# Second layer's query product: two 64-row tiles per head pair instead of one 128-row tile with a block-diagonal matrix

## The reference, cut to what matters

```python
xn = _ln(x, ln_w, ln_b)
q = softmax((xn @ Wq + bq).reshape(b, t, h, dh), axis=-1)
k = softmax((xn @ Wk + bk + (1.0 - src_mask) * -1e6).reshape(b, t, h, dh), axis=1)
v = ((xn @ Wv + bv) * src_mask).reshape(b, t, h, dh)
att = jnp.einsum('bnhd,bnhl->bhdl', k, v)          # 64 x 64 per head
y = jnp.einsum('bnhd,bhdl->bnhl', q, att).reshape(b, t, d)
scale, shift = jnp.split((silu(emb) @ W_emb + b_emb)[:, None, :], 2, axis=2)
hh = _ln(y, ln2_w, ln2_b) * (1.0 + scale) + shift
return x + silu(hh) @ W_out + b_out
```

## Time and profile before

| | us |
|---|---|
| median of 3 runs | 2306.27 |
| lowest, highest of the 3 | 2303.68, 2310.38 |
| the profiled execution, its own time | 2308.4 |
| its span, first to last instruction | 2306.6 |
| granted clock of PE over the span, share of full | 0.959 |

### The profile page before, as it was taken

The page is one execution under the profiler, slowest core; times in us unless marked ns, Lnnn a source line. Parts: engine busy times, 40 slices in busy tenths (PEclk is TensorE's granted clock), DMA queues, the critical chain, the costliest instruction groups (busy, mean ns, idle before and its releaser), DMA issues. The chain is left out here.

```text
span 2306.6 us, 30566 instructions
## 1 busy us (share of the span) xinstructions
PE 2144.4 (93%) x10240; PEld 1401.8 (61%) x10240; DVE 2044.7 (89%) x2254; ACT 1606.9 (70%) x3119; POOL 1776.2 (77%) x1046
## 2 busy tenths in 40 slices
PE   9889989988998899899979998998977899999999
PEld 3345555555555555555545555555545588888878
DVE  4899999999999999999999999999999666666666
ACT  3677787887777778777777787777656355566655
POOL 0587899999999999999999999999999522233325
PEclk9889999999999999999999999998978999999999
DMA  6611231141114111521331141114001201121113
GB/s 217 256 40 53 84 141 46 51 173 57 44 53 170 51 51 46 174 92 55 99 122 46 56 157 63 42 51 175 33 28 53 94 27 35 33 63 60 40 55 129
DMA packets 86139, 191.20 MB, mean 83 GB/s; under 512 B 8350, under 2 KB 11678, under 8 KB 85983
## 3 DMA queue, kind: packets, MB, share of 16 engines
q1 hardware_dynamic: 85982, 189.25, 24.7%
HBM read 171.91 MB, written 17.30 MB: 82 GB/s over the span
## 5 line engine op out<-in xcount | busy, mean ns | idle before, releaser
L1464 POOL TENSOR_TENSOR arena<-arena 128x1024 f32<-128x1024 f32 x512 | 1201.1, 2365 | 118.1 <-ACT arena L624 116.0
L1059 DVE TENSOR_TENSOR_SCAN arena<-ps,arena 128x512 f32<-128x512 f32 x1024 | 1235.1, 1246 | 16.4 <-ACT ps L624 13.5
L624 ACT ACTIVATE ps<-arena 128x512 f32<-128x512 f32 x1087 | 717.0, 676 | 270.9 <-DVE arena L1059 184.7
L339 PEld LDWEIGHTS ps<-keep,arena 128*128 128x128 f32 x4096 | 493.7, 147 | 262.1 <-issue 133.7
L339 PE MATMUL ps<-keep,arena 128*128 128x128 f32 x4096 | 550.3, 285 | 94.1 <-POOL arena L1464 88.4
L1044 DVE TENSOR_TENSOR arena<-ps,arena 128x1024 f32<-128x1024 f32 x407 | 487.0, 1197 | 25.3 <-PE ps L339 23.2
L278 PE MATMUL ps<-arena 128*128 128x512 f32 x1024 | 470.8, 605 | 17.8 <-issue 17.1
L278 PEld LDWEIGHTS ps<-arena 128*128 128x128 f32 x1024 | 190.3, 195 | 220.2 <-issue 219.7
L624 ACT ACTIVATE arena<-ps 128x512 f32<-128x512 f32 (+2 forms) x393 | 198.5, 538 | 135.3 <-PE ps L278 65.9
L1431 POOL TENSOR_TENSOR arena<-arena 128x1024 f32<-128x1024 f32 x105 | 248.2, 2364 | 15.1 <-PE ps L339 15.0
L624 ACT ACTIVATE arena<-arena 128x2 f32<-128x2 f32 (+4 forms) x662 | 238.3, 365 | 25.7 <-POOL arena L1408 7.5
(11 more groups left out here) (147 smaller groups left out, 2707.6 us busy)
## 6 DMA issues: line engine op xcount, KB each, us to landing
arena<-scr_bc SPq DMA_DIRECT2D x128, 512.0 KB, 7.2
arena<-in_inT SPq DMA_DIRECT2D x184, 256.0 KB, 2.7
arena<-in_x SPq DMA_DIRECT2D x17, 512.0 KB, 3.7
scr_x<-arena SPq DMA_DIRECT2D x32, 256.0 KB, 2.0
arena_b<-scr_x SPq DMA_DIRECT2D x16, 512.0 KB, 3.7
arena_c<-scr_x SPq DMA_DIRECT2D x32, 256.0 KB, 2.9
out<-arena_c SPq DMA_DIRECT2D x32, 256.0 KB, 2.1
arena<-in_x SPq DMA_DIRECT2D x30, 256.0 KB, 3.3
```

The source lines that it names most:

```text
L339: last = e.matmul(YP[:, 128 * q:128 * q + 128], hb[G % R][:, i, 128 * q:128 * q + 128], ident, start=(g == 0 and i == 0 and q == 0), stop= ...
L624: return e.activation(o_, i_, f, **kw)
L1059: e.tensor_tensor_scan(H, DA[s % 4], H, h0, MUL, ADD).then_inc(v_sc)
L1464: e.tensor_tensor(H, H, Ct[:, GN * g:GN * g + GN, :], MUL).then_inc(g_w)
```

## The change

`att` keeps only the two heads' matrices, 64 columns wide: rows 0 to 63 are the even head, rows 64 to 127 the odd head. The zeroing on POOL and its semaphore go. `attention` writes `att` in one instruction of 128 partitions where there were two of 64. `y_mm` issues two products for each `f` of a tile, one per head: 64 partitions of `qT` by 128 tokens as the stationary operand, 64 by 64 of `att` as the moving one. The heads of a pair go to different banks: one bank holds the even heads of both tiles, the other the odd heads. `y_block` scales one bank (both tiles, one parity of heads) per instruction, and waits first for both tiles' products.

```diff
-        qT, acc, att, kb = sb(4, 18 * 128), sb(4, 64), sb(4, 128), [sb(4, TB) for _ in range(2)]
+        qT, acc, att, kb = sb(4, 18 * 128), sb(4, 64), sb(4, 64), [sb(4, TB) for _ in range(2)]
             def y_mm(K):
-                e.wait_ge(v_att, 2 * (K // 8 + 1))
+                e.wait_ge(v_att, K // 8 + 1)
                 e.wait_ge(a_qT, 2 * K + 2)
+                P = [bank8(("y", K, h), (v_y, 2 * K + h + 1)) for h in range(2)]
                 for t in (2 * K, 2 * K + 1):
-                    P, at_ = bank8(("y", t), (v_y, t + 1)), 128 * (t % 18)
+                    at_, to = 128 * (t % 18), 256 * (t % 2)
                     for f in range(4):
-                        last = e.matmul(P[:, 128 * f:128 * f + 128], qT[:, f, at_:at_ + 128], att[:, f, :], start=True, stop=True)
+                        for h in range(2):
+                            head = slice(64 * h, 64 * h + 64)
+                            last = e.matmul(P[h][:, to + 64 * f:to + 64 * f + 64], qT[head, f, at_:at_ + 128], att[head, f, :],
+                                            start=True, stop=True)
                     last.then_inc(p_ya)
             def attention(b):
-                e.wait_ge(g_att, 1)
                 if b:
                     e.wait_ge(p_ya, 16)
-                for lo in (0, 64):
-                    rows_ = slice(lo, lo + 64)
-                    e.tensor_tensor(att[rows_, :, rows_], acc[rows_, :, :], ks[rows_, :].unsqueeze(2).broadcast_to([64, 4, 64]),
-                                    MUL).then_inc(v_att)
+                e.tensor_tensor(att, acc, ks.unsqueeze(2).broadcast_to([128, 4, 64]), MUL).then_inc(v_att)
             def y_block(K):
-                for n in range(2):
-                    t = 2 * K + n
-                    e.wait_ge(p_ya, t + 1)
-                    e.tensor_tensor(yt[:, n, :].rearrange("p (a b) -> p a b", a=8),
-                                    PS[bank_of["y", t]].rearrange("p (a b) -> p a b", a=8),
-                                    rq[:, t, :].unsqueeze(2).broadcast_to([128, 8, 64]), MUL).then_inc(v_y)
+                e.wait_ge(p_ya, 2 * K + 2)
+                for h in range(2):
+                    e.tensor_tensor(yt.rearrange("p n (a h b) -> p n a h b", a=4, h=2)[:, :, :, h, :],
+                                    PS[bank_of["y", K, h]].rearrange("p (n a b) -> p n a b", n=2, a=4),
+                                    rq[:, 2 * K:2 * K + 2, :].rearrange("p n (a h) -> p n a h", h=2)[:, :, :, h].unsqueeze(3)
+                                    .broadcast_to([128, 2, 4, 64]), MUL).then_inc(v_y)
-                if n == 2:
-
-                    e.wait_ge(p_op, 256)
-                    e.memset(flat(att), 0.0).then_inc(g_att)
```

More of the change, by code:

```diff
@@ L149, in program @@
         g_c, g_r1, g_r2, g_r3, g_rs, g_nm, g_dt, g_du, g_gw, g_w = (sem("g_" + n) for n in ("c", "r1", "r2", "r3", "rs", "nm", "dt", "du", "gw", "w"))
-        g_att, g_m1, g_mask, g_l1, g_l2, g_lrs, g_q, g_xo = (sem("g_" + n) for n in ("att", "m1", "mask", "l1", "l2", "lrs", "q", "xo"))
+        g_m1, g_mask, g_l1, g_l2, g_lrs, g_q, g_xo = (sem("g_" + n) for n in ("m1", "mask", "l1", "l2", "lrs", "q", "xo"))
         after = lambda k, n: ((16 * k[0] + k[1] + n) // 16, (k[1] + n) % 16)
```

## The result

| | us |
|---|---|
| changed kernel, median of 9 runs | 2312.68 (2310.79 to 2316.67) |
| before, median of 9 runs | 2306.27 (2302.68 to 2310.38) |
| ratio, 95% interval | 1.0026 (1.0017 to 1.0036) |
| span of the profiled execution, after and before | 2310.9 and 2306.6 |

The changed kernel is slower by 6.4 us by the medians (by the interval, 3.9 to 8.3 us). The forecast was 2310.4: 4.1 us slower.

A forecast was written before the change was run, and what follows sets the result against it. PE was taken as the bound in the stretch with nearly all changed calls; 12 y_mm calls on the chain at +0.29 us plus 0.6 in the last pass gave +4.1, so 2310.4 us, range 2299 to 2323.

The forecast's parts named there:

- The stream of records: y_mm on PE: 32 half-row records, pairs side by side at 0.112 us, 1.79 us in all, as today.
- B: Rival in y_mm: one load at a time, a call 3.80 us, +2.02; 2336 us in all; chance 0.14.
- D: Rival in y_mm: a load waits for the product in its own rows, a call +1.11 us; 2322 us; chance 0.08.
- C: Rival in y_mm: half the rows halve the load, a call -0.60 us; 2300 us; chance 0.09.
- The change of division: PE around each y_mm: emptying the array, going in and out, an exposed load; 0.28 us, making a call +0.29.
- The four calls in the gaps: y_mm(7) to y_mm(10), where PE sits idle for something else: the dearer calls add nothing to the end.
- The last pass: At h_tr(15), after the later y_block: PE waits about 0.6 us for ACT's normalisation, once.
- The cover in the other passes: Running passes: the later y_block is covered, as DVE sits idle 1.18 to 3.79 us for L553 before it.
- Edits that cost nothing: attention in one instruction, the dropped zeroing (0.53 us on POOL) and bank8's wait for both banks: no effect on the time.
- The sum: Whole kernel: 12 x 0.29 + 0.6 = +4.1 us, laid on the median of 2306.27: 2310.4 us.

The follow-up runs named there:

- the quarters: Changed kernel with each y_mm product cut again by tokens, loading 64 rows by 64 columns: 2300.04 us against 2307.41 for the kernel before, ratio 0.9967.
- the two filled kernels: Kernel before and changed kernel, each with three fp32 products of 512 columns added where PE waits ahead of o_mm(8): 2305.41 and 2310.45 us.

## Why the prediction was right

**The stream of records.** The forecast was 0.056 us from record to record, with both row halves side by side and nothing gained. It is 0.056, so B (0.11), D (0.08) and C (0.03) are out. This decides more than the time does: the stated range, 2299 to 2323, held C and D as well. The reason holds as well: with half the moving columns a record still costs 0.108 us, and the load binds. L256, with 2 rows and 2 moving columns, had been the row that said so the earlier trace rows, and the overlap of row halves could be taken over from the column halves of `kv_mm`.

**What the argument left out.** I wrote that the moving side had been hidden behind the weights. It is not hidden but nearly equal: with 64-column loads and 128 moving columns a pair costs 0.109 us, with 128-column loads and 64 moving columns a record 0.108. The change halved one of two equal limits. Halving both is what pays, and the quarters do that with one more cut.

**The change of division.** Forecast was a call dearer by 0.29 us. It is 0.34 in the blocks up to `y_mm(6)`, 0.33 in the passes, and 0.31 where the change of division was bought alone. Taken 12 times, this term was too small by 0.6 us of 4.1, within its bounds of 0.23 to 0.5. The four calls in the gaps added nothing, as forecast (0.92 us late at `o_mm(8)` against 0.91 before them).

**The last pass.** Forecast 0.6 us of waiting at `h_tr(15)`, measured 0.55; in the kernel that has the later start alone it is 0.72, and the stretch is longer by 0.69. The cover in the other passes held.

**Edits that cost nothing.** `attention(1)` takes 0.93 us in one instruction against 2.39 in two, and the first low part of block 7 then waits 0.87 us for ACT, so nothing was passed on. Behind 2000 us PE shows waits for DVE's low parts and for ACT alone, none for a bank.

**The sum.** By the trace, 11 x 0.34 and 0.86 are 4.6 us; forecast were 4.1. Measured were 6.4 by the medians, and 5.0 between the two filled kernels, whose profiles differ by 4.6 from the first changed call on. The interval of the first (3.9 to 8.3) holds all of these. So the forecast of the time came out 2.3 us too low: 0.5 of that is what the trace shows beyond the sum, and the other 1.8, between 4.6 and 6.4, can be chance or clock falls that come more often in one kernel than in the other. These runs do not settle which.

## What to carry to other kernels

For a small product, write down two prices for each record: its weight columns and its moving columns. In these fp32 products of up to 128 columns, tiling the array gained only when both fell; cutting one of two equal ones gave twice the records for the same time. Then count the changes of division: each, there and back, cost PE about 0.3 us here, so a tiled step has to save more than that per visit. And where a consumer is made to wait for the second of two tiles, look at the last pass: it is the one without a following step to hide the delay.

## What the runs showed of the hardware

- Four quarters of the array ran side by side: four fp32 records of 64 by 64 weights and 64 moving columns in 0.060 us, where a pair of row halves took 0.112 and one whole record 0.112.
- A record of an fp32 product costs about 0.11 us if either its weights or its moving side has 128 columns (a pair in two halves side by side costs it once). Rows do not matter: loads of 128 columns gave it with 2, 64 and 128 rows.
- Two row halves overlapped also where four products of one half stood before four of the other, though less well: 0.075 us a record over a call, 0.06 in its middle, 0.11 at its start.
- Changing how the array is divided and back cost PE 0.29 to 0.34 us with a whole step in it, and 0.31 with two records.
- After the same wait of 3.03 us, PE's clock fell to 1.2 GHz in one profile and not in two others. It also fell behind a wait of 1.88 us. At `o_mm(8)`, on the chain, a fall cost 1.3 to 2.8 us (7.07 to 8.58 against 5.76); at `o_mm(7)`, with a wait behind it, nothing.
